# The quantized Gelu chain of a feed-forward layer, two feature tiles at a time instead of one

## The reference

```
h   = round(x @ w1 + b1, to 1/256)
h   = piecewise-linear Gelu of h, 33 breakpoints 0.25 apart on [-4, 4],
      identity above, 0 below, rounded to 1/256
out = round(h @ w2 + b2, to 1/256)
y   = x + layernorm(out)
```

## Time and profile before

| | |
|---|---|
| median of 3 runs | 1228.38 us (1227.55 to 1300.74) |
| the profiled execution, its own time | 1228.59 us |
| its span on the slowest core (core 6) | 1227.1 us |
| spans of the 8 cores | 1222.7 to 1227.1 us |
| PE busy | 1139.3 us (93%) |
| ACT busy | 983.1 us (80%) |
| DVE busy | 751.6 us (61%) |
| POOL busy | 180.9 us (15%) |

### The profile page before, as it was taken

The page is one execution under the profiler, slowest core; times in us unless marked ns, Lnnn a source line. Parts: engine busy times, 40 slices in busy tenths (PEclk is TensorE's granted clock), DMA queues, the critical chain, the costliest instruction groups (busy, mean ns, idle before and its releaser), DMA issues.

```text
span 1227.1 us, 26972 instructions; the slowest of 8 cores (1222.7 to 1227.1 us)
## 1 busy us (share of the span) xinstructions
PE 1139.3 (93%) x11162; PEld 640.9 (52%) x11298; DVE 751.6 (61%) x1613; ACT 983.1 (80%) x1217; POOL 180.9 (15%) x357
## 2 busy tenths in 40 slices
PE   2889989999999999999998899879999999999996
PEld 2565556666565666666564444434444444444443
DVE  7876533333434324343344589996888888888843
ACT  3449999999999999999999578887777777777720
POOL 4530010010100100000002243430111111111110
PEclk9999999999999999999999999989999999999999
DMA  9952532343433412111119965656333333333211
GB/s 260 268 158 59 96 72 52 70 83 66 84 57 61 79 34 44 38 23 32 28 36 198 219 219 155 161 118 150 112 112 112 112 112 121 120 122 111 77 69 69
DMA packets 62870, 128.00 MB, mean 104 GB/s; under 512 B 9238, under 2 KB 26134, under 8 KB 62108
## 3 DMA queue, kind: packets, MB, share of 16 engines
q1 hardware_dynamic: 53900, 101.10, 28.2%
q0 software_dynamic: 8848, 25.17, 13.6%
HBM read 117.84 MB, written 25.17 MB: 117 GB/s over the span
## 4 chain that ended last, share of the span: by engine, by line
PE 73%; DVE 13%; ACT 8%; DMA 3%; issue 2%; POOL 1%; SPq 0%; DVEq 0%; POOLq 0%; ACTq 0%
PE pW L948 18%; PE pF L875 14%; PE pjb L316 11%; PE S L409 9%; PE acc L462 9%; PE pjb L348 8%; ACT P L425 6%; DMA xst<-x_full 2%; PE pja L316 1%; DVE x L578 1%; DVE bst L235 1%; DVE bst L236 1%; DVE g L919 1%; DVE kst L326 1%; DVE g L913 1%
## 5 line engine op out<-in xcount | busy, mean ns | idle before, releaser
L425 ACT ACTIVATE P<-S,biasT 128x1024 bf16<-128x1024 f32 (+1 forms) x576 | 563.4, 1078 | 20.9 <-PE S L409 19.1
L875 PE MATMUL pF<-xl2T,w1s 128*128 128x512 bf16 x1002 | 257.7, 384 | 12.3 <-ACT cu L890 11.0
L948 PE MATMUL pW<-w2s,hq 128*128 128x512 bf16 x1003 | 250.8, 380 | 3.3 <-ACT pW L973 2.2
L462 PEld LDWEIGHTS acc<-V,P 128*128 128x128 bf16 x4352 | 162.6, 97 | 53.5 <-DVE ctx L480 11.3
L462 PE MATMUL acc<-V,P 128*128 128x66 bf16 x4352 | 179.1, 193 | 4.1 <-DVE ctx L480 2.4
L409 PE MATMUL S<-Q,K 64*128 64x512 bf16 (+3 forms) x1280 | 173.4, 349 | 8.4 <-ACT P L425 6.6
L875 PEld LDWEIGHTS pF<-xl2T,w1s 128*128 128x128 bf16 x1024 | 100.2, 99 | 132.1 <-ACT cu L890 12.8
L948 PEld LDWEIGHTS pW<-w2s,hq 128*128 128x128 bf16 x1024 | 100.3, 98 | 123.9 <-issue 3.9
L316 PE MATMUL pjb<-xlT,W 128*128 128x512 bf16 x572 | 152.3, 381 | 13.0 <-issue 6.5
L326 DVE CAST kst<-pjb 128x512 bf16<-128x512 f32 x81 | 56.0, 691 | 132.5 <-PE pjb L316 128.7
L890 ACT ACTIVATE cu<-pF,b1s 128x512 int32<-128x512 f32 x128 | 87.7, 685 | 59.2 <-PE pF L875 59.2
(11 more groups left out here) (91 smaller groups left out, 1064.9 us busy)
## 6 DMA issues: line engine op xcount, KB each, us to landing
w1s<-w1bf SPq DMA_DIRECT2D x128, 256.0 KB, 2.7
xst<-x_full SPq DMA_DIRECT2D x32, 512.0 KB, 9.8
K<-kst SPq DMA_DIRECT2D x128, 64.0 KB, 2.0
Q<-kst SPq DMA_DIRECT2D x128, 64.0 KB, 2.3
w1bf<-w POOLq DMA_DIRECT2D x32, 256.0 KB, 4.0
x<-x_full SPq DMA_DIRECT2D x16, 512.0 KB, 5.2
w2s<-w POOLq DMA_DIRECT2D x8, 1024.0 KB, 26.9
x2scr<-x SPq DMA_DIRECT2D x16, 512.0 KB, 4.2
```

The lines of the kernel that those rows point to most:

```text
L425: t = put("scalar", lambda io: io.activation(out=P3[:, :, c0:512], in_=S[s][:].rearrange("p (o c) -> p o c", o=2)[:, :, c0:512], func=AF.E ...
L462: io.matmul(acc[:, q * 66:(q + 1) * 66], P[p][:, at:at + 128], zv[:, o, j, hh, :], start=st, stop=sp, skip_group_check=True),
L875: t = put("tensor", lambda io, c=c: io.matmul(pF[b][:], w1s[n % 4][:, c * 128:(c + 1) * 128], xl2T3[g][:, c, :], start=(c == 0), stop=(c = ...
L948: t = put("tensor", lambda io, ft=ft, hf=hf: io.matmul(pO[b][:, hf * 512:(hf + 1) * 512], slot_of(g, ft, tl), w2s[:, ft * 1024 + hf * 512: ...
```

## The change

A pair m is the feature tiles 2m and 2m+1. `u` still takes one bank at a time, and writes one half of a buffer of 1024 columns. The split, the Gelus, the difference, the product and the sum then run once for the pair, on 1024 columns, and `hq` again once for each tile.

Three kinds of buffers of 1024 columns are left, three of each. `cu` takes the integers, and `r` is written over them, which now waits for `s`. `cs` takes the breakpoints; `g1` is written over them, then the difference and the product. `cg` takes `g0`, and the sum is written over it. So `u` waits for `m` of three pairs back, the split for `y` of three pairs back, and `g0` for the `hq` of three pairs back. `y` now waits for `m` of its own pair, and `m` for `d` just before it.

```diff
-    cu, cs, cr = chain("cu", 2, I32), chain("cs", 3, I32), chain("cr", 4, I32)
-    g0, g1, cy = chain("g0_", 4, F32), chain("g1_", 4, F32), chain("cy", 2, I32)
+    two = lambda nm_, n: [sb(f"{nm_}{i}", 1024, I32, slots.pop(0)) for i in range(n)]
+    cu, cs, cg = two("cu", 3), two("cs", 3), two("cg", 3)
+    f32 = lambda b: b[:].bitcast(F32)
...
         def f_u(n):
-            ft, b, k = order[n][1], pf(n), n % 2
+            ft, b, m = order[n][1], pf(n), n // 2
             F[n, "u"] = put("scalar", lambda io: io.activation(
-                out=cu[k][:], in_=pF[b][:], func=AF.Identity, bias=b1s[:, ft:ft + 1], scale=256.0),
-                after=[F[n, "mm"], F.get((n - 2, "r"), t_ctx)], inc=True)
+                out=cu[m % 3][:, n % 2 * 512:n % 2 * 512 + 512], in_=pF[b][:], func=AF.Identity,
+                bias=b1s[:, ft:ft + 1], scale=256.0), after=[F[n, "mm"], F.get((m - 3, "m"), t_ctx)], inc=True)
...
+        def f_split(m):
+            u, k = m % 3, m % 3
+            F[m, "s"] = put("vector", lambda io: io.tensor_scalar(
                 out=cs[k][:], in0=cu[u][:], scalar1=-64, scalar2=None, op0=ALU.bitwise_and),
+                after=[F[2 * m, "u"], F[2 * m + 1, "u"], F.get((m - 3, "y"))], inc=True)
+            F[m, "r"] = put("vector", lambda io: io.tensor_scalar(
+                out=cu[u][:], in0=cu[u][:], scalar1=63, scalar2=None, op0=ALU.bitwise_and),
+                after=[F[m, "s"]], inc=True)
+
+        def f_g0(m):
+            k = m % 3
+            F[m, "g0"] = put("scalar", lambda io: io.activation(
+                out=f32(cg[k]), in_=cs[k][:], func=AF.Gelu, bias=0.0, scale=1.0 / 256),
+                after=[F[m, "s"], t_hq.get(2 * m - 5)], inc=True)
+
+        def f_g1(m):
+            k = m % 3
+            F[m, "g"] = put("scalar", lambda io: io.activation(
+                out=f32(cs[k]), in_=cs[k][:], func=AF.Gelu, bias=q25[:], scale=1.0 / 256),
+                after=[F[m, "g0"]], inc=True)
+
+        def f_d(m):
+            k = m % 3
+            F[m, "d"] = put("vector", lambda io: io.tensor_tensor(
+                out=f32(cs[k]), in0=f32(cs[k]), in1=f32(cg[k]), op=ALU.subtract),
+                after=[F[m, "g"]], inc=True)
+
+        def f_m(m):
+            k = m % 3
+            F[m, "m"] = put("vector", lambda io: io.scalar_tensor_tensor(
+                out=f32(cs[k]), in0=cu[k][:], scalar=4.0, in1=f32(cs[k]), op0=ALU.mult, op1=ALU.mult),
+                after=[F[m, "r"], F[m, "d"]], inc=True)
+
+        def f_y(m):
+            k = m % 3
+            F[m, "y"] = put("vector", lambda io: io.scalar_tensor_tensor(
+                out=cg[k][:], in0=f32(cg[k]), scalar=256.0, in1=f32(cs[k]), op0=ALU.mult, op1=ALU.add),
+                after=[F[m, "m"]], inc=True)
 
         def f_hq(n):
             g, ft = order[n]
-            a = [F[n, "y"]] + ([C[ft // 2, "left"]] if g == 0 else left[g, ft // 8])
-            src = cy[n % 2][:].rearrange("p (t c) -> p t c", t=4)
+            m = n // 2
+            a = [F[m, "y"]] + ([C[ft // 2, "left"]] if g == 0 else left[g, ft // 8])
+            src = cg[m % 3][:, n % 2 * 512:n % 2 * 512 + 512].rearrange("p (t c) -> p t c", t=4)
...
         def chain_step(n, g):
             has = lambda i: 0 <= i < len(order)
-            if has(n - 2):
-                f_g(n - 2)
-            if has(n - 3):
-                f_d(n - 3)
-            if has(n - 4):
-                f_y(n - 4)
-            if has(n - 3):
-                f_m(n - 3)
-            if has(n - 5):
-                f_hq(n - 5)
+            m = n // 2
+            if has(2 * m - 2):
+                (f_g1 if n % 2 else f_g0)(m - 1)
+            if has(n - 6):
+                f_hq(n - 6)
+            if has(2 * m - 4):
+                if n % 2:
+                    f_y(m - 2)
+                else:
+                    f_d(m - 2)
+                    f_m(m - 2)
             if has(n):
                 f_u(n)
-                f_split(n)
+                if n % 2:
+                    f_split(m)
...
         def fin(n):
-            for i in range(1, 6):
+            for i in range(1, 7):
                 chain_step(n + i, order[n][0])
```

More of the change, by code:

```diff
@@ L170, in build_nc @@
     w1s = [sb(f"w1s{i}", 1024, BF16, R3 + (62 + 2 * i) * K) for i in range(4)]
-    slots = [R3 + (24 + i * 2) * K for i in range(19)]
-    chain = lambda nm_, n, ty: [sb(f"{nm_}{i}", 512, ty, slots.pop(0)) for i in range(n)]
-    cu, cs, cr = chain("cu", 2, I32), chain("cs", 3, I32), chain("cr", 4, I32)
-    g0, g1, cy = chain("g0_", 4, F32), chain("g1_", 4, F32), chain("cy", 2, I32)
+    slots = [R3 + (24 + i * 4) * K for i in range(9)]
+    two = lambda nm_, n: [sb(f"{nm_}{i}", 1024, I32, slots.pop(0)) for i in range(n)]
+    cu, cs, cg = two("cu", 3), two("cs", 3), two("cg", 3)
+    f32 = lambda b: b[:].bitcast(F32)
     assert max(end_b, R3 + 78 * K) <= 229368, max(end_b, R3 + 78 * K)
@@ L893, in f_u @@
             pFfree[b] = F[n, "u"]
-        def f_split(n):
-            u, k, kr = n % 2, n % 3, n % 4
-            F[n, "s"] = put("vector", lambda io: io.tensor_scalar(
+        def f_split(m):
+            u, k = m % 3, m % 3
+            F[m, "s"] = put("vector", lambda io: io.tensor_scalar(
                 out=cs[k][:], in0=cu[u][:], scalar1=-64, scalar2=None, op0=ALU.bitwise_and),
-                after=[F[n, "u"], F.get((n - 3, "g"))], inc=True)
-            F[n, "r"] = put("vector", lambda io: io.tensor_scalar(
-                out=cr[kr][:], in0=cu[u][:], scalar1=63, scalar2=None, op0=ALU.bitwise_and), inc=True)
```

## The result

The changed kernel takes 1232.63 us (median of 7 runs) against 1228.38 before; the ratio is 1.0032, with a 95% interval of 1.0021 to 1.0043. That is within 2%, and inside the forecast range of 1221 to 1236 us, but it is not "no change": it is 4.2 us slower, where I forecast 0.2. On the chip that ran e5 to e8 half of the cores were slowed in every execution, so for those four kernels I give the mean span of the other four cores, with a standard error of 0.2 to 0.3 us; it is 1224.6 us there for the kernel before, and on the other chips 1224.8 us before and 1228.4 us after the change.

What follows compares the result with a forecast made beforehand. PE bounds the kernel except in group 0, where VectorE's queue is the clock from about 747 us to the last `c_x2`. Terms -1.3 - 1.2 + 2.7 = +0.2 us gave 1228.8 on the profiled execution, 1228.6 as median; range 1221 to 1236.

Steps and rivals of the forecast that it cites:

- groups 1 to 3: The 96 tiles after group 0: PE's 6.91 us a pair covers ScalarE's 5.05 and VectorE's 5.9, so no cost.
- the drain: Last hq before the second layer needs tile 30 at 1174.6 us: ends at 1172.4, hidden by 2 us.
- the fourth rival: In-place r loses the double rate, 0.53 us more in each pair: +8, 1236 us; chance 0.03.
- VectorE's queue: VectorE's operations in group 0, the clock there after 747 us: three terms, -1.3 - 1.2 + 2.7 = +0.2 us.
- dry pair: Pair in group 0 where VectorE runs out of work: three forecast, 0.7, 1.0 and 1.0 us.
- The lock-step: Group 0: g0 waits for s, which waits for u; VectorE runs dry in three pairs, +2.7 us.
- The ramp: End of group 0: one tile's d and m move into group 1, -1.2 us, or 0 if PE takes it back.
- The saving in own work: VectorE in group 0: a pair costs 4.87 us including neighbour waits, 0.09 less; -1.3 us over 14 pairs.
- The handover at 820 us: From group 0 to the second layer: xl waits for POOL, PE for xl, 3.84 us; costs nothing.
- the second rival: g0's wait for s becomes group 0's clock: about 1240 us, or 1234 with half the pairs; chance 0.20.
- The first: Rival for group 0: neighbour waits cost nothing and dry pairs are covered, -6.1 us, 1222.5 us; chance 0.22.
- The third: Rival for groups 1 to 3: the lock-step passes PE's 6.91 us a pair, +24 us, 1253; chance 0.03.

Runs made afterwards that it cites:

- e5: Changed kernel with ScalarE's even step ordered hq, u, g0 instead of g0, hq, u; 1227.1 us mean span of four cores.
- e8: Changed kernel with u ahead of g0, r between d and m, and token-tile parts over 29 steps instead of 32; 1224.3 us mean span.
- e4: Changed kernel with VectorE reordered so no operation waits for its neighbour: d, r, m in even steps, s, y in odd; 1249.45 us, ratio 1.0167.
- e2: Kernel before the change, with m issued directly behind d instead of y between them; 1231.17 us, ratio 1.0022.
- e6: Changed kernel with r moved between d and m, y still ahead of s; 1226.6 us mean span of four cores.
- e3: Changed kernel with only the VectorE operations beside the last POOL chain of group 0 split into halves; 1231.83 us, ratio 1.0028.

## Why the prediction was right or wrong

**The bound, the durations, groups 1 to 3, the drain: right.** `d`, `m` and `y` take 1205 to 1225 ns, `s` and `r` 691 to 694; an in-place `r` keeps its rate, so the fourth rival falls. PE's 130 of 130 us, the 329.6 us (329.9 before) and the 56.1 us (as before) show that all the work behind the chain stayed hidden. At the drain it stayed hidden by less than the 2 us that I worked out: on core 3 the second layer is alone from 1161.42 us, so by 0.216 us a matmul it comes to tile 30 at 1174.4, and the last two `hq` start at 1173.55 and end at 1174.7, not 1172.4. That PE's pace was not safe by itself, e4 shows: the margin is used up when every `y` stands behind an `s`.

**VectorE's queue: the sum was wrong, 0.2 for 1.9 us.** It had three terms. Three operations and a dry pair of the changed kernel (core 3) show the prices:

```profile
784.05 1.22 DVE L919 TENSOR_TENSOR cs<-cs,cg 128x1024 f32<-128x1024 f32 x1
785.30 1.23 DVE L925 SCALAR_TENSOR_TENSOR cs<-cu,cs 128x1024 f32<-128x1024 int32 x1
786.56 1.23 DVE L931 SCALAR_TENSOR_TENSOR cg<-cg,cs 128x1024 int32<-128x1024 f32 x1
788.73 0.69 DVE L898 TENSOR_SCALAR cs<-cu 128x1024 int32<-128x1024 int32 x1 [0.94 <-ACT cu L891]
```

The lock-step (+2.7) was right in kind and nearly in size: of the three pairs that I laid out as dry, two were, with 0.94 us each for a forecast of 1.0; steps 16 and 17 were not. Two more waits, of 0.17 and 0.91, came at the first two pairs. Together `s` waits for `cu` 3.0 us. The ramp (-1.2) did not come. Those early waits, 1.1 us, are about its size and are probably where it went, as the text allowed ("0 if PE takes it back"). The saving in own work (-1.3) did not come either: a neighbour wait cost 0.12 instead of 0.10, as e2 and the changed kernel show (`m` 1.25 us after `d`, where an operation that does not wait starts after 1.14). It is there twice in every pair and a third time in 5 of the 11 pairs in the middle of group 0, 0.28 to 0.29 us on average. An operation without a wait takes 0.61 or 1.14 us, which makes 4.64 for a pair and saves 0.32. From the residual at 728 us (726 after) to the last, the queue took 1.8 us more, just what the two dry pairs are (1.9); without them it is as long as before within 0.1 us. So nearly all of the fixed cost that the change was to save went back into the waits that its order created; e6 takes two of them out and gains 3.0 us.

**POOL: the step that failed most plainly.** "The handover at 820 us ... only moves with VectorE" was false. I named the POOL chain as a link, but gave it no term in the sum, as if it kept the duration of before. It grew from 2.99 to 4.90 us with VectorE's operations, and e3 shows that they are the cause. That is 1.9 us, as much as the whole error of VectorE's queue. The trace of before had the sign: the same operation (`rs`, L242) takes 0.21 us at 709 us, beside VectorE's statistics of one input, and 0.54 in group 0 beside the chain. The Trainium skill, "SBUF — State Buffer", section "SBUF: two separate sides", has the rule: VectorE (in a two-port mode, or with two SBUF inputs against a GpSimd operation that reads SBUF) and GpSimd share a port pair that one of them locks for a whole instruction. The traces agree in that the four operations take 0.53 to 0.87 us beside operations of 0.68 us, and 0.66 to 1.53 beside 1.22; a lock itself no trace shows.

**The number.** The measured 1232.6 us is 4.0 above the 1228.6 of the forecast. So it lies outside the 3 us that I gave a chance of 0.52, and so do the 122.1 us from the first matmul of group 0 to the first of the second layer (118.5 before), which were to keep their length within 3 us. It is inside 1221 to 1236 us because I had drawn the range up to 1236 for another mechanism, the half-way form of the second rival, at 1234 us. That the range held was luck as far as POOL's 1.9 us go, for no rival had them.

**The rivals.** The first (waits are free) is refuted by e2. The second (lock-step in most pairs) is refuted by the waits' count, 4 in group 0, of which one is 0.17 us. The third was not seen in the change; e4 shows what it warned of, by another loop.

## What to carry to other kernels

Merging two tiles into one wider operation saves a fixed cost per operation, here about 0.06 us on VectorE, but look first at what stood between dependent operations: a wait for the direct neighbour costs 0.12 us, and two or three of them in a pair ate what its five operations saved. Longer VectorE operations also lengthened the tiny POOL operations beside them, and a chain of four of them on the critical path paid four times. In an in-order queue ask of each moved operation what waits behind it: putting each `y` behind an `s` cost 17 us, where the same edit gained 2.0 in VectorE's stretch.

## What was unexpected in the hardware

The same POOL operation on one column (`rs`, L242 or L243, core 3) mostly took 0.21 us beside VectorE's statistics, 0.54 beside the chain of 512 columns, and 1.07 or 1.64 beside that of 1024. An earlier start of a PE stretch can be given back with the clock: in e3 the second layer began 1.6 us earlier, on core 3 some 8 us at 0.53 to 0.62 of the full clock followed where the changed kernel had 1.00, and over the 8 cores the stretch behind it was 1.5 us longer at the median. A VectorE operation that waits for the one just ahead of it started 0.12 us later than one that does not, at 512 columns and at 1024.
